# Probabilities times V for four query tiles in one slot instead of a quarter in each of four

## Chip, cores and metric

One core of one Trainium2 chip. The metric is the device time of one execution in microseconds (us).

## What is computed

`x` is [8, 1024, 512] in float32: eight batches ("b") of 1024 tokens. The block has two halves. The first is attention on the normalised input, with a residual:

```python
xn = layernorm(x)
qk = (xn @ W_qk + b_qk).reshape(b, s, 8, 64, 2);  q, k = qk[..., 0], qk[..., 1]
v = (xn @ W_v + b_v).reshape(b, s, 8, 64)
attn = softmax(einsum('bihd,bjhd->bhij', q, k) * 64 ** -0.5)
o = einsum('bhij,bjhd->bihd', attn, v).reshape(b, s, 512)
x = x + (layernorm(o @ W_out + b_out) * gamma + beta + xn) * 2 ** -0.5
```

The second half normalises x again, mixes each token with the one before it, and computes `sigmoid(xr @ W_r.T) * (relu(xk @ W_k.T) ** 2 @ W_v.T)`, which is added to x. The change touches only the line with `attn` times `v`.

## The kernel before, in words

Two passes stand one behind the other: `attention_pass` (L60 to L629), which leaves the attention output in DRAM (`o_scratch`), and `mix_pass` (from L632), which does the rest in chunks of 512 tokens. The change lies in the attention pass. Each engine has its own hand-written program, and semaphores tie them together; a `wait_ge` holds everything behind it on its engine.

The attention pass runs a loop over the batches (seven turns of `entry(b, False)` and one last `entry(B - 1, True)`). A batch is a row of slots, n = 0 to 69 (`LAST_SLOT` is 70). Slot n belongs to head h = n // 8 and has r = n % 8. There are 8 heads with 8 query tiles of 128 tokens each, so slots 0 to 63 each make the scores of one tile, and the slots behind them finish. In slot n, TensorE (PE) does in this order:

- `scores(b, n)` (L503): 4 matmuls of 512 columns into one of two score buffers `ps_scores`, each two PSUM banks wide. It waits until the exponential of tile n - 2 has read the buffer (`exp_done`), and at r = 0 for the head's q and k.
- in slots 55 to 58 and 62 to 65 (`XHAT_TURNS`), except in the last batch, the transposes of one tile of the next batch's normalised input, `turn_xhat` (L458), through `ps_misc`. They wait for the readers of what ps_misc held before (`misc_free_of_qk`, `misc_free_of_xhat`).
- in the first slots of a batch the products for V, `project_v` (L497).
- at r = 3 `spread_inv` (L544): transposes of the reciprocal row sums of the head before, through `ps_misc`. At n = 66 that of the last head, through the bank of `ps_turnA`, behind that slot's products.
- `turn_probs(b, n - 2)` (L518): eight transposes of the probabilities of tile n - 2, four into `ps_turnA` and four into `ps_turnB`. Each half waits until the bank was copied out for the tile before (`turnA_stored`, `turnB_stored`).
- `p_at_v` (L528): probabilities times V. Four query tiles make a "quad"; quad number `quad` covers the tiles 4 * quad to 4 * quad + 3 and needs all four turned. For each of the 8 key tiles (jt) there are two matmuls of 64 output rows and 256 columns, one per half of the array's columns; two tiles share one of them. They accumulate in `ps_o`, whose left half takes the head's first quad (q2 = 0) and its right half the second (q2 = 1). The before-kernel calls it in every slot from n = 6 on with part = (n - 6) % 4 and does 2 of the 8 key tiles each time. The first part waits for the turned probabilities, and at q2 = 0 for `o_done`, that VectorE has read `ps_o` for the head before.
- `project_qk` (L464): pieces of the q and k projection of the next head, 4 matmuls at r = 7, 0 and 1, 6 matmuls at r = 3 and 4, none at r = 2, 5 and 6. The piece at r = 3 waits (L603) until `inv_cols` was copied out of `ps_misc`. Heads 6 and 7 have none in slots 55 to 58; the next batch's first head is projected in slots 59, 60 and 65.

VectorE (DVE) does in slot n: the row maximum of the scores of tile n (L330), at r = 1 the reciprocal of the row sums and its widening (L337, L339), at r = 2 the rests of k and q (L290, L296), at r = 5 that of k and at r = 6 that of q, in the xhat slots `xT_lo` (L283), then the copy of `ps_turnB` (tile n - 2) into `probsT` (L357), in slots 38 to 45 statistics of the next batch (L261), in slots 52, 53 and the xhat slots `normalise` (L277), and last, at r = 5 and h >= 1, the product `oT = ps_o * inv_cols` of the head before (L376), which waits for `pv_done`.

ScalarE (ACT) does in slot n: the exponential of tile n - 1 (L433, with its row sum), at r = 2 and 5 the copies of q and k (L402, L403), in the xhat slots `xT_hi` (L396), the copy of `ps_turnA` (tile n - 2) into `probsT` (L445), and at r = 3 the copy of the spread reciprocals into `inv_cols` (L411); for the last head this stands at n = 66. At a batch's end PE waits for that copy (L624) and for `turnB_stored` (L625) before its loop turns.

`probsT` has room for two quads. SyncE's queue copies k between partition halves (L186, L187), stores oT (L192) and loads the next x.

Of the kernel before, what the change touches and what calls it, by code (L numbers as in the profile page):

```python
# [27 lines left out]
TT = T // P  # L28
# [11 lines left out]
QUAD = 4  # L40
# [19 lines left out]
def attention_pass(nc, x, w_qk, b_qk, w_v, b_v, w_out, w_r, w_out_raw, stage, o_scratch, ln1_stats, ident):  # L60
    with ExitStack() as ctx:
# [3 lines left out]
        def sem(name):  # L65
            return ctx.enter_context(nc.semaphore(name))
# [84 lines left out]
        turnA_stored = sem("turnA_stored")  # L151
        turnB_stored = sem("turnB_stored")
# [5 lines left out]
        o_done = sem("o_done")  # L158
# [6 lines left out]
        with nc.Block() as block:  # L165
# [291 lines left out]
            def _(pe):  # L457
                def turn_xhat(b, t, turned):  # L458
                    pe.wait_ge(xhat_done, 8 * b + t + 1)
                    for k in range(KC):  # L460
                        ins = pe.transpose(turned[:, k, :], xhat[t % 2][:, k * P:(k + 1) * P], ident[:, :])
                    ins.then_inc(xhatT_done, 1)
# [13 lines left out]
                def misc_free_of_qk(b, h, half):  # L476

                    pe.wait_ge(qk_hi_done, 16 * b + 2 * h + half + 1)
                    pe.wait_ge(qk_lo_done, 16 * b + 2 * h + half + 1)

                def misc_free_of_xhat(b, t):
                    pe.wait_ge(xT_hi_done, 8 * b + t + 1)
                    pe.wait_ge(xT_lo_done, 8 * b + t + 1)
# [13 lines left out]
                def project_v(b, t):  # L497
                    prods = [(xt, w, kc) for kc in range(KC) for xt, w in ((xT_lo, wv_hi), (xT_hi, wv_lo), (xT_hi, wv_hi))]
                    for i, (xt, w, kc) in enumerate(prods):
                        ins = pe.matmul(v_banks[t], xt[:, kc, t * P:(t + 1) * P], w[:, kc, :], start=(i == 0), stop=(i == 11))  # L500
                    ins.then_inc(v_done, 1)

                def scores(b, n):  # L503
                    h, r = n // TT, n % TT
                    if r == 0:
                        pe.wait_ge(qk_lo_done, 16 * b + 2 * h + 2)
                        pe.wait_ge(k_copied[h % 2], 128 * b + 32 * (h // 2) + 32)
                    if n >= 2:
                        pe.wait_ge(exp_done, 64 * b + n - 1)
                    tile = slice(query_tile(r) * P, (query_tile(r) + 1) * P)  # L510
                    for half in range(2):
                        cols = slice(half * HALF, (half + 1) * HALF)
                        for i, k in enumerate((k_lolo, k_hihi)):
                            ins = pe.matmul(ps_scores[n % 2][:, cols], q_hilo[h % 2][:, tile], k[h % 2][:, cols],  # L514
                                            start=(i == 0), stop=(i == 1))
                    ins.then_inc(scores_done, 1)
# [8 lines left out]
                            ins = pe.transpose(ps[:, j, :], probs[m % 3][:, (first + j) * P:(first + j + 1) * P], ident[:, :])  # L525
                        ins.then_inc(done, 1)

                def p_at_v(b, quad, part):  # L528

                    h, q2 = quad // 2, quad % 2  # L530
                    if part == 0:
                        pe.wait_ge(turnA_stored, 64 * b + QUAD * quad + QUAD)
                        pe.wait_ge(turnB_stored, 64 * b + QUAD * quad + QUAD)
                        if q2 == 0 and h >= 1:
                            pe.wait_ge(o_done, 8 * b + h)
                    for jt in (2 * part, 2 * part + 1):
                        for half in range(2):
                            ins = pe.matmul(ps_o[half * DH:(half + 1) * DH, q2 * 2 * P:(q2 + 1) * 2 * P],  # L538
                                            v[:, jt, h * DH:(h + 1) * DH], probsT[:, quad % 2, jt, half, :],
                                            start=(jt == 0), stop=(jt == TT - 1))  # L540
                    if part == 3 and q2 == 1:
                        ins.then_inc(pv_done, 1)

                def spread_inv(b, h, turned=ps_misc[:, :]):  # L544
# [7 lines left out]
                def entry(b, last):  # L552
                    for n in range(LAST_SLOT):
                        h, r = n // TT, n % TT
                        if n == 0:
                            project_v(b, 0)
                            project_v(b, 1)
                        if n < SLOTS:
                            scores(b, n)
                        if not last and n in XHAT_TURNS:  # L560
                            t = XHAT_TURNS.index(n)
                            if t == 0:
                                misc_free_of_qk(b, HEADS - 1, 1)
                            elif t == 4:
                                misc_free_of_qk(b + 1, 0, 0)
                            else:
                                misc_free_of_xhat(b + 1, t - 1)
                            turn_xhat(b + 1, t, misc4)
                        for t in range(TT):
                            if V_SLOTS[t] == n and n > 0:  # L570
                                if t in (2, 4, 5, 6, 7):

                                    pe.wait_ge(v_stored, 8 * b + (1 if t == 2 else t))
                                project_v(b, t)
                        if r == 3 and 1 <= h < HEADS:
                            if h < HEADS - 1:
                                misc_free_of_qk(b, h + 1, 0)
                            elif last:
                                misc_free_of_qk(b, h, 1)
                            else:  # L580
                                misc_free_of_xhat(b + 1, 3)
                            spread_inv(b, h - 1)
                        if n == 2:
                            pe.wait_ge(v_stored, 8 * b + 3)
                        if 2 <= n < SLOTS + 2:
                            turn_probs(b, n - 2)
                        if n == 6:
                            pe.wait_ge(v_stored, 8 * b + TT)
                        if n >= 6:
                            p_at_v(b, (n - 6) // QUAD, (n - 6) % QUAD)  # L590

                        if h < HEADS - 1:
                            if n == 0:
                                misc_free_of_qk(b, 0, 1)
                                project_qk(b, 1, 0, 0, 4)
                            if r == 0:
                                project_qk(b, h + 1, 0, 4, 8)
                            if r == 1:
                                project_qk(b, h + 1, 0, 8, 12)
                            if r == 3:  # L600
                                misc_free_of_qk(b, h + 1, 0)
                                if h >= 1:
                                    pe.wait_ge(inv_stored, 8 * b + h)  # L603
                                project_qk(b, h + 1, 1, 0, 6)
                            if r == 4:
                                project_qk(b, h + 1, 1, 6, 12)
                            if r == 7 and h < HEADS - 2:
                                misc_free_of_qk(b, h + 1, 1)
                                project_qk(b, h + 2, 0, 0, 4)
                        if not last:  # L610

                            if n == 59:
                                pe.wait_ge(inv_stored, 8 * b + h)
                                project_qk(b + 1, 0, 0, 0, 6)
                            if n == 60:
                                project_qk(b + 1, 0, 0, 6, 12)
                            if n == 65:
                                misc_free_of_xhat(b + 1, TT - 1)
                                project_qk(b + 1, 0, 1, 0, 12)
                        if n == SLOTS + 2:  # L620
                            pe.wait_ge(turnA_stored, 64 * b + SLOTS)
                            spread_inv(b, HEADS - 1, turnA_bank)
                        if n == LAST_SLOT - 1 and not last:
                            pe.wait_ge(inv_stored, 8 * b + HEADS)  # L624
                            pe.wait_ge(turnB_stored, 64 * b + SLOTS)  # L625

                with pe.Fori(0, B - 1) as b:
                    entry(b, False)
                entry(B - 1, True)  # L629


# [525 lines left out]
```

## Time and profile before

| | |
|---|---|
| time, median of 3 runs | 3000.94 us (3000.56 to 3002.95) |
| span of the profiled execution, first to last instruction | 2998.2 us |
| PE busy | 2890.0 us, 96% |
| weight loads (beside PE) | 2168.0 us, 72% |
| DVE busy | 2068.8 us, 69% |
| ACT busy | 1572.7 us, 52% |
| DMA, hardware queue | 14.6% of 16 engines |
| instructions | 44311 |

The span is that of one execution; its whole time was not taken apart from the three runs, whose median lies 2.7 us above it. PE's busy time counts from the start of a matmul to its modelled end, and matmuls overlap, so a busy PE may still be waiting for an array that drains. A line of the timeline is one instruction, or several of one kind in a row (xN); the number in brackets is idle time before it and what ended it.

### The profile page before, as it was taken

The numbers are of one execution on the slowest core, as the hardware profiler recorded it, in microseconds if no ns is written. First come the engines' busy times: TensorE is split into PE (matmuls) and PEld (weight loads), VectorE is DVE, ScalarE is ACT, GpSimd is POOL, SyncE is SP. The second block draws the span as 40 slices with busy tenths as digits, with TensorE's granted clock in tenths as the row PEclk, the third lists the DMA queues.
The fourth block names the chain that finished last, engine by engine and source line by source line (L and its number), as shares of the span: only waits on it lengthen the run. The fifth ranks groups of instructions, "written<-read, shape, count | busy, mean of one in ns | idle before, by whom it ended". The sixth has DMA issues, their size and how long they took to land. (4 is left out here: it accounts for less than half of the span.)

```text
span 2998.2 us, 44311 instructions
## 1 busy us (share of the span) xinstructions
PE 2890.0 (96%) x16432; PEld 2168.0 (72%) x16432; DVE 2068.8 (69%) x2885; ACT 1572.7 (52%) x2553; POOL 278.5 (9%) x227
## 2 busy tenths in 40 slices
PE   7999999999999999999999999999969999999999
PEld 5777777777777777777777777777747777777777
DVE  5667566656756665675666566666668898989896
ACT  3555455455535555554555455455545555555453
POOL 2000000000000000000000000000013333233332
PEclk9999999999999999999999999999979999999999
DMA  3101110111011111111110111111131111111110
GB/s 102 50 22 26 33 47 22 33 32 40 22 37 36 33 34 32 30 32 26 47 24 23 39 40 25 23 29 50 26 98 57 70 59 66 63 63 66 59 70 29
DMA packets 61407, 128.62 MB, mean 43 GB/s; under 512 B 8464, under 2 KB 8464, under 8 KB 61200
## 3 DMA queue, kind: packets, MB, share of 16 engines
q1 hardware_dynamic: 61200, 125.86, 14.6%
q8 instruction: 130, 2.13, 0.3%
q14 instruction: 77, 0.63, 0.1%
HBM read 58.73 MB, written 33.55 MB: 31 GB/s over the span
## 5 line engine op out<-in xcount | busy, mean ns | idle before, releaser
L330 DVE TENSOR_REDUCE neg_max<-ps_scores 128x1 f32<-128x1024 f32 x512 | 625.0, 1221 | 601.5 <-PE ps_scores L514 601.4
L433 ACT ACTIVATE probs<-ps_scores,neg_max 128x1024 f32<-128x1024 f32 x512 | 571.3, 1116 | 219.3 <-DVE neg_max L330 218.9
L445 ACT ACTIVATE probsT<-ps_turnA 128x512 f32<-128x512 f32 x512 | 305.4, 597 | 572.2 <-PE ps_turnA L525 569.6
L538 PE MATMUL ps_o<-probsT,v 128*64 128x256 f32 x4096 | 551.3, 391 | 4.0 <-DVE oT L376 2.5
L514 PE MATMUL ps_scores<-k_lolo,q_hilo 128*128 128x512 f32 x1024 | 423.9, 414 | 1.0 <-DMA k_lolo<-k_lolo 1.0
L514 PE MATMUL ps_scores<-k_hihi,q_hilo 128*128 128x512 f32 x1024 | 401.5, 392 | 0.0
L538 PEld LDWEIGHTS ps_o<-probsT,v 128*64 128x64 f32 x4096 | 251.0, 136 | 164.9 <-issue 83.7
L357 DVE COPY probsT<-ps_turnB 128x512 f32<-128x512 f32 x512 | 350.7, 685 | 10.9 <-PE ps_turnB L525 4.8
L525 PE MATMUL ps_turnB<-ident,probs 128*128 128x128 f32 x2048 | 308.1, 273 | 0.5
L525 PE MATMUL ps_turnA<-ident,probs 128*128 128x128 f32 x2048 | 306.5, 272 | 0.0
L525 PEld LDWEIGHTS ps_turnA<-ident,probs 128*128 128x128 f32 x2048 | 250.6, 140 | 53.7 <-issue 0.8
L514 PEld LDWEIGHTS ps_scores<-k_lolo,q_hilo 128*128 128x128 f32 x1024 | 191.9, 187 | 113.7 <-issue 77.7
L525 PEld LDWEIGHTS ps_turnB<-ident,probs 128*128 128x128 f32 x2048 | 238.9, 141 | 3.2 <-DVE probsT L357 2.3
L471 PE MATMUL ps_misc<-xT_hi,wqk_lo 128*128 128x512 f32 x508 | 219.9, 433 | 1.5 <-DVE xT_lo L283 1.5
L514 PEld LDWEIGHTS ps_scores<-k_hihi,q_hilo 128*128 128x128 f32 x1024 | 192.5, 188 | 33.7
L471 PE MATMUL ps_misc<-xT_lo,wqk_hi 128*128 128x512 f32 x508 | 205.9, 405 | 0.0
L471 PE MATMUL ps_misc<-xT_hi,wqk_hi 128*128 128x512 f32 x508 | 205.7, 405 | 0.0
L237 POOL TENSOR_TENSOR rstd<-mean_var,eps 128x8 f32<-128x8 f32 x8 | 1.6, 201 | 1810.6 <-DVE mean_var L265 1810.6
L402 ACT ACTIVATE q_hilo<-ps_misc,bqk 64x512 fp32r<-64x512 f32 x127 | 86.9, 684 | 146.6 <-PE ps_misc L471 145.7
L471 PEld LDWEIGHTS ps_misc<-xT_hi,wqk_lo 128*128 128x128 f32 x508 | 95.8, 189 | 77.2 <-issue 60.8
L1060 PE MATMUL bank<-mix_wv_hi,act_lo 128*128 128x512 f32 x256 | 104.6, 409 | 28.6 <-DVE act_lo L867 20.8
L290 DVE SCALAR_TENSOR_TENSOR k_lolo<-ps_misc,bqk,k_hihi 64x512 fp32r<-64x512 f32 x127 | 96.1, 757 | 41.3 <-ACT k_hihi L403 37.5
(175 smaller groups left out, 4602.5 us busy)
## 6 DMA issues: line engine op xcount, KB each, us to landing
stage<-in_L_attn_x_dram SPq DMA_DIRECT2D x32, 512.0 KB, 4.3
k_hihi<-k_hihi SPq DMA_DIRECT2D x64, 256.0 KB, 2.9
k_lolo<-k_lolo SPq DMA_DIRECT2D x64, 256.0 KB, 3.9
o_scratch<-oT SPq DMA_DIRECT2D x128, 128.0 KB, 3.1
stage<-o_scratch SPq DMA_DIRECT2D x16, 1024.0 KB, 5.6
xc<-in_L_attn_x_dram SPq DMA_DIRECT2D x16, 1024.0 KB, 5.2
out_dram<-gate SPq DMA_DIRECT2D x64, 256.0 KB, 2.1
probsT<-in_L_attn_W_qk_dram SPq DMA_DIRECT2D x4, 512.0 KB, 8.4
```

What stands on the lines that cost most here:

```text
L237: pool.tensor_tensor(rstd[:, :], mean_var[:, :, 1], eps[:, :], ALU.add).then_inc(eps_done, 1)
L290: dve.scalar_tensor_tensor(k_lolo[i][DH:P, cols], ps[DH:P, :], bqk[DH:P, h:h + 1], f32(k_hihi[i][DH:P, cols]), ALU.add, ALU.subtract).then ...
L330: dve.tensor_reduce(neg_max[:, h % 2, r:r + 1], ps_scores[n % 2][:, :], AX_X, ALU.max, negate=True).then_inc(max_done, 1)
L357: dve.tensor_copy(probsT[:, m // QUAD % 2, 4:8, m % 2, m % QUAD // 2 * P:(m % QUAD // 2 + 1) * P], ps_turnB[:, :, :]).then_inc(turnB_store ...
L402: act.activation(q_hilo[i][0:DH, cols], ps[0:DH, :], ACT.Identity, bias=bqk[0:DH, h:h + 1])
L433: act.activation(probs[m % 3][:, :], ps_scores[m % 2][:, :], ACT.Exp, bias=neg_max[:, m // TT % 2, m % TT:m % TT + 1], accum_out=row_sum[: ...
L445: act.activation(probsT[:, m // QUAD % 2, 0:4, m % 2, m % QUAD // 2 * P:(m % QUAD // 2 + 1) * P], ps_turnA[:, :, :], ACT.Copy).then_inc(tu ...
L471: ins = pe.matmul(ps[:, :], w[:, kc, h, :, :].rearrange("p s d -> p (s d)"), xt[:, kc, cols], start=(n == 0), stop=(n == 11))
L514: ins = pe.matmul(ps_scores[n % 2][:, cols], q_hilo[h % 2][:, tile], k[h % 2][:, cols], start=(i == 0), stop=(i == 1))
L525: ins = pe.transpose(ps[:, j, :], probs[m % 3][:, (first + j) * P:(first + j + 1) * P], ident[:, :])
L538: ins = pe.matmul(ps_o[half * DH:(half + 1) * DH, q2 * 2 * P:(q2 + 1) * 2 * P], v[:, jt, h * DH:(h + 1) * DH], probsT[:, quad % 2, jt, hal ...
L1060: ins = pe.matmul(out, a[:, kc, a_cols], b[:, kc, b_cols], start=(i == 0), stop=(i == len(prods) - 1))
```

## The change

The four calls of `p_at_v` for a quad become one, in the slot of the first: all 8 key tiles, 16 matmuls, at n = 6, 10, 14, ... 66. The waits stay the same and stand ahead of it. `pv_done` now rises in slot r = 2 instead of r = 5. No other instruction is added, removed or moved, and no buffer changes. At n = 66 `spread_inv` now stands behind the whole of the last quad.

```diff
-                def p_at_v(b, quad, part):
+                def p_at_v(b, quad):
 
                     h, q2 = quad // 2, quad % 2
-                    if part == 0:
-                        pe.wait_ge(turnA_stored, 64 * b + QUAD * quad + QUAD)
-                        pe.wait_ge(turnB_stored, 64 * b + QUAD * quad + QUAD)
-                        if q2 == 0 and h >= 1:
-                            pe.wait_ge(o_done, 8 * b + h)
-                    for jt in (2 * part, 2 * part + 1):
+                    pe.wait_ge(turnA_stored, 64 * b + QUAD * quad + QUAD)
+                    pe.wait_ge(turnB_stored, 64 * b + QUAD * quad + QUAD)
+                    if q2 == 0 and h >= 1:
+                        pe.wait_ge(o_done, 8 * b + h)
+                    for jt in range(TT):
                         for half in range(2):
                             ins = pe.matmul(ps_o[half * DH:(half + 1) * DH, q2 * 2 * P:(q2 + 1) * 2 * P],
                                             v[:, jt, h * DH:(h + 1) * DH], probsT[:, quad % 2, jt, half, :],
                                             start=(jt == 0), stop=(jt == TT - 1))
-                    if part == 3 and q2 == 1:
+                    if q2 == 1:
                         ins.then_inc(pv_done, 1)
...
-                        if n >= 6:
-                            p_at_v(b, (n - 6) // QUAD, (n - 6) % QUAD)
+                        if n >= 6 and (n - 6) % QUAD == 0:
+                            p_at_v(b, (n - 6) // QUAD)
```

## Rows read from the trace of the kernel before

**Rows 1.** The page, part 1: busy us, share of the span, instructions.
```profile
PE 2890.0 (96%) x16432; PEld 2168.0 (72%) x16432; DVE 2068.8 (69%) x2885; ACT 1572.7 (52%) x2553; POOL 278.5 (9%) x227
```

**Rows 2.** Table of stretches, one batch: us, busy us per engine, PE clock, DMA.
```profile
340.00:610.00 270.00, 266.95 (x1634) 194.48 (x1633) 170.36 (x226) 143.82 (x242) 1.83 (x2) 1.00 0.13 32
```

**Rows 3.** The page, part 5: the products of probabilities and V on PE.
```profile
L538 PE MATMUL ps_o<-probsT,v 128*64 128x256 f32 x4096 | 551.3, 391 | 4.0 <-DVE oT L376 2.5
```

**Rows 4.** Timeline, slots 5 and 6 of a head: start us, us, engine, line.
```profile
731.38 0.39 PE L514 MATMUL ps_scores<-k_lolo,q_hilo 128*128 128x512 f32 x1
...
732.49 1.23 DVE L330 TENSOR_REDUCE neg_max<-ps_scores 128x1 f32<-128x1024 f32 x1 [2.57 <-PE ps_scores L514]
...
732.73 0.60 PE L525 MATMUL ps_turnB<-ident,probs 128*128 128x128 f32 x4
...
733.25 1.08 PE L538 MATMUL ps_o<-probsT,v 128*64 128x256 f32 x8
733.75 0.76 DVE L290 SCALAR_TENSOR_TENSOR k_lolo<-ps_misc,bqk,k_hihi 64x512 fp32r<-64x512 f32 x1
...
734.54 0.69 DVE L357 COPY probsT<-ps_turnB 128x512 f32<-128x512 f32 x1
734.60 0.39 PE L514 MATMUL ps_scores<-k_hihi,q_hilo 128*128 128x512 f32 x1
...
735.26 0.69 DVE L376 TENSOR_TENSOR oT<-ps_o,inv_cols 128x512 f32<-128x512 f32 x1
...
736.26 0.44 PE L538 MATMUL ps_o<-probsT,v 128*64 128x256 f32 x2
```

**Rows 5.** Timeline of PE, a slot without such a block.
```profile
337.28 0.60 PE L525 MATMUL ps_turnB<-ident,probs 128*128 128x128 f32 x4
...
337.95 0.40 PE L471 MATMUL ps_misc<-xT_lo,wqk_hi 128*128 128x512 f32 x1
```

**Rows 6.** Timeline, slot 3 of a head and the start of slot 4.
```profile
721.94 0.50 PE L514 MATMUL ps_scores<-k_lolo,q_hilo 128*128 128x512 f32 x1
...
724.65 0.59 ACT L411 ACTIVATE inv_cols<-ps_misc 128x512 f32<-128x512 f32 x1
...
725.50 0.50 PE L471 MATMUL ps_misc<-xT_hi,wqk_lo 128*128 128x512 f32 x1
...
726.99 0.39 PE L514 MATMUL ps_scores<-k_lolo,q_hilo 128*128 128x512 f32 x1
```

**Rows 7.** Timeline of DVE, slot 56.
```profile
534.39 0.68 DVE L283 TENSOR_TENSOR xT_lo<-ps_misc,xT_hi 128x512 fp32r<-128x512 f32 x1
...
535.59 0.54 DVE L277 TENSOR_SCALAR xhat<-stage,mean_var,rstd 128x512 f32<-128x512 f32 x1
```

**Rows 8.** Timeline, the start of slot 46's block.
```profile
496.20 0.67 DVE L376 TENSOR_TENSOR oT<-ps_o,inv_cols 128x512 f32<-128x512 f32 x1
...
497.02 1.08 PE L538 MATMUL ps_o<-probsT,v 128*64 128x256 f32 x8 [0.36 <-DVE oT L376]
```

**Rows 9.** Timeline, slot 66 to the next batch's first matmul.
```profile
569.72 1.08 PE L538 MATMUL ps_o<-probsT,v 128*64 128x256 f32 x8
...
570.73 0.66 PE L549 MATMUL ps_turnA<-ident,inv_wide 128*128 128x128 f32 x4
...
571.32 2.81 PE L538 MATMUL ps_o<-probsT,v 128*64 128x256 f32 x24
571.42 0.60 ACT L411 ACTIVATE inv_cols<-ps_turnA 128x512 f32<-128x512 f32 x1 [0.22 <-PE ps_turnA L549]
...
576.45 0.47 PE L500 MATMUL ps_turnA<-wv_hi,xT_lo 128*128 128x512 f32 x1 [2.33 <-issue]
```

**Rows 10.** Stretches behind the attention pass (columns as in rows 2), and PE's timeline there.
```profile
2177.00:2180.00 3.00, 0.38 (x4) 0.00 (x0) 0.69 (x1) 0.00 (x0) 0.00 (x0) 1.00 0.21 49
2189.00:2194.00 5.00, 5.00 (x13) 3.73 (x13) 0.92 (x5) 0.00 (x0) 0.00 (x0) 0.50 1.05 397
...
2188.66 0.76 PE L1060 MATMUL bank<-mix_wout_hi,o_lo 128*128 128x512 f32 x1 [11.28 <-DVE o_lo L838]
```

## The prediction

> **What bounds the kernel now.** First the page's busy times: TensorE (PE) is busy for 2890 of 2998.2 us, VectorE (DVE) for 69%, ScalarE (ACT) for 52% [rows 1]. Then the table of stretches: in one batch of the attention pass PE is busy for 266.95 of 270 us at a granted clock of 1.00 [rows 2]. So the attention pass (7 x 269 us and a shorter last batch) is bound by PE, and PE's slots set the beat. But a busy PE need not be doing work: the timeline shows what a block of products of probabilities and V costs beside its columns. Last I read who is how late behind PE in the slots where the block now disappears: DVE's chain there [rows 4] and ACT's [rows 6]. I call a slot by r = n mod 8.
>
> **A quarter block and its switch.** With a block, the second matmul of the next slot starts 734.60 - 732.73 = 1.87 us after the first transpose into turnB [rows 4]; in a slot without one, 337.95 - 337.28 = 0.67 us later [rows 5]. A block costs PE 1.20 us. Its work is less: the stretch of 24 records takes 2.81 us, one of 8 takes 1.08 [rows 9], so a further pair of records (the two halves run side by side) takes 1.73 / 8 = 0.216 us, and a block's four pairs 0.86. The other 0.34 us is paid for going into the 64-column form and out again. The page has 4096 records [rows 3], 8 to a block: 512 blocks, 128 quads. A quad in one go costs PE 1.20 + 12 x 0.216 = 3.79 us, not 4.80: 1.01 less. If PE alone counted, that were 128 x 1.01 = 129 us, less a little at the batch ends.
>
> The work now lies in slots r = 2 and r = 6 (2.59 us longer), and slots 0, 1, 3, 4, 5, 7 are 1.20 us shorter. What used to pass under their blocks comes into view, slot by slot.
>
> **Slots 5 and 6.** Let slot 5 begin at 0 (731.38). DVE: row maximum 1.11 to 2.34, k rest 2.37 to 3.13, copy of turnB 3.16 to 3.85, the product into oT (L376) 3.88 to 4.57 [rows 4]. This chain starts from the slot's own scores and does not get shorter. PE's next product block writes the ps_o that L376 reads, and waits for it (o_done); today it starts at 4.88, just after, so nobody is seen to wait. Without the block in slot 5, PE would reach it at 1.35 (turnB) + 0.67 + 3 x 0.23 + 0.44 + 0.52 = 3.67. It can't start before 4.57 + 0.15 = 4.72; the 0.15 is from the place where this wait already shows, 496.87 to 497.02 [rows 8]. So of 1.20 us only 0.16 are gained. What is queued behind the wait on PE is the whole block and slot 7; DVE and ACT catch up meanwhile. In slots 45 and 53 of a batch a further DVE instruction stands ahead of L376, so the wait shows today already (slot 46's block is the one in [rows 8]), and the gain is 0.
>
> **Slot 3.** The projection's second half overwrites ps_misc, which ACT reads for inv_cols (L411). ACT ends it at 725.24, 3.30 us after the slot's start; the projection starts at 3.56 today [rows 6], with the block in between. Without it PE is ready at about 2.4, but waits until 3.30 less 0.08 (the transposes of inv_wide no longer wait for the q rest of slot 2) plus 0.15: 3.37. Gain 0.19, with a shorter start-up 0.21, not 1.20. Slots 4, 7, 0 and 1 keep their whole 1.20: maximum and copy (1.23 + 0.69) fit into slots of 2.7 us or more, and the scores' round trip (2.4 us to the end of maximum and exponential behind the scores) fits into two slots.
>
> **A head.** From the block of r = 2 to that of r = 6: +2.59 - 0.21 - 1.20 - 0.16 = +1.02 us. From r = 6 to r = 2: 2.59 - 3 x 1.20 = -1.01. A head is unchanged. Per batch, quads 0 to 12 (the first gap is of the cheap kind): -6 x 1.01 + 6 x 1.02 + 2 x 0.16 = +0.4 us.
>
> **Slots 55 to 66, next batch's xhat.** These slots have no projection, and each turns a tile of xhat through ps_misc. PE without the block needs 0.92 + 0.44 + 0.87 = 2.23 us; DVE needs 1.14 + 0.60 + 0.60 + 0.57 = 2.9 (maximum, xT_lo, copy, normalise [rows 7]), and some 0.57 more in slot 57. Over 55 to 57 DVE falls 9.3 - 6.7 = 2.6 us behind; the two score banks absorb part. Following xT_lo to the next transpose I get a wait of 0.45 in slot 57 and 1.1 in slot 58: +0.6 net between slots 55 and 59 instead of -1.0. Slots 59 and 60: -0.2 and -1.2. Slot 61 stores k and q rests, so its DVE chain is 0.8 longer and sets the next block's start today already: 0. Slots 63 to 65: transpose, ACT's xT_hi, DVE's xT_lo, next transpose is a round trip of some 2.1 us, beside a PE need of 1.31 in slots 64 and 65, so the three give back only 0.9 of 3.6. With the two blocks' extra 2.59 each (quads 12 and 14): +0.6 - 1.4 + 5.2 - 0.9 = +3.5. Bounds: 0 lost to these waits gives -0.8; all of DVE's lag and of the round trips in view gives +4.5. I take +3.5, from following the chain.
>
> **The batch's end.** Today a quarter block at 569.72 is followed by the transposes of inv_wide at 570.73, ACT copies them from 571.42 to 572.02, and three quarters (571.32 to 574.13) run meanwhile; PE's stream waits for that copy (L624), turns the loop, and the next batch's first matmul is at 576.45, with 2.33 us idle on "issue" [rows 9]. That is 4.43 us after the copy. Now the transposes stand behind the whole quad: copy's end at 3.29 + 0.31 + 0.66 + 0.04 + 0.60 = 4.9 us after the block's start, not 2.3. If the loop's turn runs from the wait's release, the next batch starts 2.6 us later; if it runs from the last matmul (2.3 us after it), 4.9 + 2.3 against 6.7: 0.5 later. I take 2.6, as the idle time has no other releaser and the sequencer is ahead of the array.
> By the Trainium skill (Runtime: NRT & Kernel Launch, Instruction fetch mechanics) a taken branch whose target is not held forces a fetch before execution goes on. By that rule the turn's price hangs on when the branch is reached, and the 2.6 stands; no run here shows the fetch itself yet.
>
> **Sum.** A batch with a successor: +0.4 + 3.5 + 2.6 = +6.5 us less roundings, say +6.3; seven of them 44 us. The last batch has no xhat and no loop turn: its slots 55 to 61 keep most of their gain and the end is 0.5 later; 0 within 3 us. The mix pass is untouched. Against the profiled span 2998.2 this is 3042; the medians lie 2.7 above the span (3000.94), so 3045.
>
> **Rivals.**
> 1. PE alone sets the time (faster). The waits of slots 3 and 6 don't bind: then 7 x (1.04 + 0.99) more is gained in each of 8 batches, about 110 us: 2935; and with the xhat slots and the ends free as well, 2872. It decides at one point: if L376 were over 3.5 us after slot 5 begins. Against it: four DVE instructions behind the scores sum to 3.4 us whatever PE does [rows 4].
> 2. The clock falls. PE is idle at the seven batch ends for over 4 us instead of 2.3. After the attention pass comes an idle time of 11.28 us: the clock is 1.00 in its first 3 us, and 0.50 when PE resumes, with 13 matmuls in 5 us [rows 10], 0.38 us each instead of 0.23: 2 us lost each time. 14 us, to 3059. For it: the longer idle time; against: it is nearer to 2.3 than to 11.
> The Trainium skill (TensorE: Matmul & The Clock Gate, Why this matters for your kernels) tells to avoid idle gaps between bursts of matmuls for this reason. By that rule this edit is worse than the sum says; the trace agrees only in that 11.28 us were too long.
> 3. The price at xhat and at the ends is half of mine: 3045 - 7 x (1.5 + 1.5) = about 3024.
> 4. It balances out: the two waits a little shorter (0.3 us each) give 3045 - 8 x 7 x 0.6 = 3011, and with rival 3 below 3000. This is the "same" case.
>
> **How the numbers follow.** Forecast 0.57, rival 2 0.15, rival 3 0.10, rival 4 0.08, rival 1 0.10. A measurement of this kernel can tell 0.2%, 6 us, from no change. The range goes from rival 4 (3011, taken as 3012) to rival 2 with turns of the loop 2 us dearer still (3059 + 7 x 2 = 3073, taken as 3075). Faster 0.11, same 0.07, slower 0.82.
>
> **What would show it.** In the new profile PE busy falls by far more than the span changes; L538 has 128 groups of 32 records. PE waits appear: the block of r = 6 for L376 (about 1 us, 7 per batch), the projection of slot 3 for L411 (about 1 us, 7 per batch), transposes of xhat for L283 in slots 57, 58, 64, 65. The gap between batches rises from 2.3 to over 4 us. Wrong if PE's idle time in an ordinary head is under 1.5 us, if the first matmul of a batch follows its last one as closely as today, or if the granted clock drops inside the attention pass.

## The result, and the profile after

The changed kernel takes 3056.44 us (median of 4 runs, 3054.43 to 3057.02), the kernel before 3000.75 us in the same comparison. The ratio is 1.0181, 95% interval 1.0166 to 1.0195: 55.7 us slower. The forecast was 3045, from 3012 to 3075.

The page of the changed kernel: the span, then part 1 (busy us, share, instructions), then two groups of part 5 (busy, mean ns of one, idle before and its releaser).

```profile
span 3054.2 us, 44311 instructions
...
PE 2808.2 (92%) x16432; PEld 2224.8 (73%) x16432; DVE 2079.4 (68%) x2885; ACT 1557.1 (51%) x2553; POOL 278.6 (9%) x227
...
L537 PE MATMUL ps_o<-probsT,v 128*64 128x256 f32 x4096 | 470.3, 382 | 15.7 <-DVE oT L376 14.8
...
L471 PE MATMUL ps_misc<-xT_hi,wqk_lo 128*128 128x512 f32 x508 | 216.4, 426 | 50.9 <-ACT inv_cols L411 45.0
```

The instructions are the same in number. PE is busy 81.8 us less than in [rows 1] and the products 81.0 us less than in [rows 3], though the edit leaves out nothing but switches; and the span is 56 us longer. So PE's work became cheaper and its idle time grew by more than the whole saving. The list of waits says where. Its columns: engine, line, what it waited for, us in total, times, longest.

```profile
PE ps_misc L471 <- ACT inv_cols L411: 45.0, 55, 0.8
PE ps_turnB L525 <- DVE probsT L357: 28.6, 49, 0.6
PE ps_turnA L500 <- issue: 28.0, 6, 4.8
...
PE ps_misc L461 <- DVE xT_lo L283: 19.2, 28, 0.9
...
PE ps_o L537 <- DVE oT L376: 14.8, 48, 0.8
...
PE ps_misc L461 <- DVE q_hilo L296: 9.2, 7, 1.4
PE ps_misc L471 <- DVE xT_lo L283: 5.9, 8, 1.5
```

Read it by the counts. 55 is seven heads in each of seven batches and six in the last: the projection of slot 3, which waits for inv_cols. 48 are six heads in eight batches (49 with one more place): the block of r = 6, which waits for the copy of turnB and then for the product into oT (0.6 and 0.3 us a place). 28 is four xhat slots in seven batches. 7 is slot 62. 6 is the loop's turn: seven batches have a successor, but the seventh leaves the loop instead of turning it. Idle time is counted from the modelled end of the matmul before, so a sum of these times is less than what the waits cost.

The timeline of the changed kernel, slots 3 to 7 of the head that [rows 6] and [rows 4] show before (start us, duration us, engine, line):

```profile
738.93 0.50 PE L514 MATMUL ps_scores<-k_lolo,q_hilo 128*128 128x512 f32 x1
...
740.83 0.60 PE L525 MATMUL ps_turnB<-ident,probs 128*128 128x128 f32 x4
...
741.52 0.59 ACT L411 ACTIVATE inv_cols<-ps_misc 128x512 f32<-128x512 f32 x1
...
742.26 0.47 PE L471 MATMUL ps_misc<-xT_hi,wqk_lo 128*128 128x512 f32 x1 [0.83 <-ACT inv_cols L411]
...
743.73 0.40 PE L514 MATMUL ps_scores<-k_lolo,q_hilo 128*128 128x512 f32 x1
...
746.91 0.40 PE L514 MATMUL ps_scores<-k_lolo,q_hilo 128*128 128x512 f32 x1
...
750.08 0.69 DVE L357 COPY probsT<-ps_turnB 128x512 f32<-128x512 f32 x1
...
750.80 0.69 DVE L376 TENSOR_TENSOR oT<-ps_o,inv_cols 128x512 f32<-128x512 f32 x1
750.83 0.66 PE L525 MATMUL ps_turnB<-ident,probs 128*128 128x128 f32 x4 [0.59 <-DVE probsT L357]
...
751.64 3.67 PE L537 MATMUL ps_o<-probsT,v 128*64 128x256 f32 x32 [0.15 <-DVE oT L376]
...
755.24 0.50 PE L514 MATMUL ps_scores<-k_lolo,q_hilo 128*128 128x512 f32 x1
```

Slot 3 lasts 743.73 - 738.93 = 4.80 us against 5.05 before: 0.25 gained where a quarter block of 1.20 has left. Slot 4 lasts 3.18 against 4.39: the whole 1.20. From the start of slot 5 to the block of r = 6 it is 751.64 - 746.91 = 4.73 us against 4.88: 0.15 gained of 1.20. The block takes 755.24 - 751.64 = 3.60 us to the next scores.

The batch's end in the changed kernel's timeline, and below it two stretches (length, busy us by engine, granted clock, DMA):

```profile
580.49 3.67 PE L537 MATMUL ps_o<-probsT,v 128*64 128x256 f32 x32
...
584.09 0.66 PE L548 MATMUL ps_turnA<-ident,inv_wide 128*128 128x128 f32 x4
584.78 0.60 ACT L411 ACTIVATE inv_cols<-ps_turnA 128x512 f32<-128x512 f32 x1 [2.81 <-PE ps_turnA L548]
...
589.30 0.77 PE L500 MATMUL ps_turnA<-wv_hi,xT_lo 128*128 128x512 f32 x1 [4.55 <-issue]
```

```profile
588.00:596.00 8.00, 6.70 (x17) 5.28 (x18) 0.69 (x1) 0.00 (x0) 0.00 (x0) 0.57 0.35 92
596.00:604.00 8.00, 8.00 (x36) 6.48 (x35) 3.14 (x3) 2.28 (x4) 0.00 (x0) 1.00 0.00 0
```

The copy of inv_cols ends 4.89 us after the block began, where [rows 9] give 2.30. The next batch follows 3.92 us after the copy (4.43 in [rows 9]), 8.81 after the block began instead of 6.73. And PE resumes at the lower of its two clock levels: 0.57 on average over 8 us, 17 matmul starts, where the next 8 us hold 36 at 1.00.

The turn in [rows 9] is the slowest of its kernel. From the end of the copy to the next batch's first matmul the six turns before take 3.69 to 4.43 us, 3.90 on average, and those of the changed kernel 3.90 to 4.21, 4.03 on average. The trace has a record of the branch itself, on PE's sequencer (ns shortest/median/longest, first and last start in us), in the kernel before:

```profile
L627 PEldq COMPARE_BRANCH  x7: 83/3521/4151, 303.0 to 1918.5; - x7
```

and in the changed one:

```profile
L626 PEldq COMPARE_BRANCH  x7: 83/3698/3924, 308.6 to 1974.5; - x7
```

The one of 83 ns leaves the loop. The first of the kernel before starts 0.1 us after the copy of its batch ends (302.86), though three quarters of the last quad still run then; in the changed kernel the record at 585.5 starts 0.1 us after the copy (585.38) too, and PE has nothing left to run.

The starts in PE's timeline cut each batch in four. "Block" stands for the first product of probabilities and V in a slot. The numbers are us, added up over the seven batches with a successor; the forecast's are those ahead of its "less roundings":

| from, to | forecast difference | before | changed | difference |
|---|---|---|---|---|
| first V matmul, block of slot 6 | 0 | 275.7 | 287.8 | +12.1 |
| block of slot 6, block of slot 54 | +2.8 | 1271.7 | 1270.9 | -0.8 |
| block of slot 54, block of slot 66 | +24.5 | 295.2 | 321.4 | +26.2 |
| block of slot 66, next first V matmul | +18.2 | 41.6 | 58.7 | +17.1 |

Together they are +54.6 of the 55.7 us. The first row is the clock's. No wait was added in these slots. Behind each of the loop's six turns the stretch takes 39.2 us before and 40.5 to 42.0 in the changed kernel; in the first batch, which has no turn ahead of it, it takes 40.4 in both. For the batches that start at 576.45 and 589.30 its end is (the kernel before, then the changed one)

```profile
615.66 1.08 PE L538 MATMUL ps_o<-probsT,v 128*64 128x256 f32 x8
```

```profile
631.32 3.67 PE L537 MATMUL ps_o<-probsT,v 128*64 128x256 f32 x32
```

39.21 and 42.02 us after the start.

### The profile page after: what moved, and what is told of

Same layout as the page of the kernel before. It is cut to its first block and busy times, and to the rows that moved or that the text cites. A ratio compares the mean times of both kernels' runs of the same rounds, so it can differ in the third digit from the quotient of the medians.

```text
span 3054.2 us, 44311 instructions
## 1 busy us (share of the span) xinstructions
PE 2808.2 (92%) x16432; PEld 2224.8 (73%) x16432; DVE 2079.4 (68%) x2885; ACT 1557.1 (51%) x2553; POOL 278.6 (9%) x227
## 5 line engine op out<-in xcount | busy, mean ns | idle before, releaser
L537 PE MATMUL ps_o<-probsT,v 128*64 128x256 f32 x4096 | 470.3, 382 | 15.7 <-DVE oT L376 14.8
L537 PEld LDWEIGHTS ps_o<-probsT,v 128*64 128x64 f32 x4096 | 303.9, 137 | 150.2 <-issue 39.3
L357 DVE COPY probsT<-ps_turnB 128x512 f32<-128x512 f32 x512 | 351.2, 686 | 14.3 <-PE ps_turnB L525 4.0
L525 PE MATMUL ps_turnB<-ident,probs 128*128 128x128 f32 x2048 | 310.6, 274 | 29.2 <-DVE probsT L357 28.6
L471 PE MATMUL ps_misc<-xT_hi,wqk_lo 128*128 128x512 f32 x508 | 216.4, 426 | 50.9 <-ACT inv_cols L411 45.0
L471 PE MATMUL ps_misc<-xT_hi,wqk_hi 128*128 128x512 f32 x508 | 205.0, 404 | 0.0
L471 PE MATMUL ps_misc<-xT_lo,wqk_hi 128*128 128x512 f32 x508 | 204.4, 402 | 0.0
L471 PEld LDWEIGHTS ps_misc<-xT_hi,wqk_lo 128*128 128x128 f32 x508 | 96.2, 189 | 76.5 <-issue 49.9
L1059 PE MATMUL bank<-mix_wout_hi,o_lo 128*128 128x512 f32 x256 | 103.2, 403 | 23.5 <-DVE o_lo L837 12.0
```

Source lines behind the costliest of these rows:

```text
L357: dve.tensor_copy(probsT[:, m // QUAD % 2, 4:8, m % 2, m % QUAD // 2 * P:(m % QUAD // 2 + 1) * P], ps_turnB[:, :, :]).then_inc(turnB_store ...
L471: ins = pe.matmul(ps[:, :], w[:, kc, h, :, :].rearrange("p s d -> p (s d)"), xt[:, kc, cols], start=(n == 0), stop=(n == 11))
L1059: ins = pe.matmul(out, a[:, kc, a_cols], b[:, kc, b_cols], start=(i == 0), stop=(i == len(prods) - 1))
```

## The experiments

Each run was timed in turn with the kernel before. Theory A is the prediction's: a slot that loses its quarter block is held by the chain behind it, if there is one. Theory B: a quad in one go costs the same everywhere. Theory C: PE saves everywhere, and the loss is at the batch ends alone.

| run | what it is | us | ratio to before, 95% |
|---|---|---|---|
| after | the change | 3056.4 | 1.0181 (1.0166 to 1.0195) |
| e1_even | quads 0, 2, ... 10 in one go | 2957.3 | 0.985 (0.9833 to 0.9866) |
| e2_odd | quads 1, 3, ... 11 | 3058.2 | 1.0181 (1.0164 to 1.0198) |
| e3_xhat | quads 12, 13, 14 | 3032.4 | 1.0097 (1.0077 to 1.0118) |
| e4_tail | quad 15 | 3031.3 | 1.0093 (1.0076 to 1.011) |
| e5_tail_first | after, inv_wide turned ahead of the last quad | 3025.9 | 1.0079 (1.0063 to 1.0096) |
| e6_inv_first | after, inv_cols copied first in slot 3 | 3006.0 | 1.001 (1.0001 to 1.002) |
| e7_vector | after, new order on DVE in slot 5 | 3015.3 | 1.0043 (1.0026 to 1.006) |
| e8_both | e6 and e7 | 2965.4 | 0.9878 (0.9861 to 0.9894) |
| e9b_heads_both | e8, quads 12 to 15 in quarters | 2913.5 | 0.9704 (0.9688 to 0.972) |
| e10b_before_orders | before, with the new orders | 3008.5 | 1.002 (1.001 to 1.0029) |
| e11_not_slot61 | e9b, slot 61 in its old order | 2914.7 | 0.9701 (0.9687 to 0.9714) |
| e12_last_quad_too | e11 and quad 15 as in e5 | 2910.8 | 0.9692 (0.9679 to 0.9705) |

### The change in four parts

```diff
+WHOLE = [0, 2, 4, 6, 8, 10]      # e2: [1, 3, ... 11]   e3: [12, 13, 14]   e4: [15]
...
-                        if n >= 6:
-                            p_at_v(b, (n - 6) // QUAD, (n - 6) % QUAD)
+                        if n >= 6:
+                            quad, part = (n - 6) // QUAD, (n - 6) % QUAD
+                            if quad not in WHOLE:
+                                p_at_v(b, quad, part, part + 1)
+                            elif part == 0:
+                                p_at_v(b, quad, 0, 4)
```

`p_at_v(b, quad, part, end)` does the key tiles 2 * part to 2 * end - 1.

Even quads. 

> Only quads 0, 2, 4, 6, 8 and 10 of each batch are made in one go (slots 6, 14, ... 46); all others in quarters as before. Theory A (each slot that loses its quarter is held by the chain that stands behind it): here slots 7, 0 and 1 are shortened, where nothing is late, and slot 5 keeps its quarter, so every one of the 48 quads saves the full 1.01 us: 3001 - 48 = 2952 us. Theory B (a quad in one go costs the same everywhere, +55.7 us / 128 = +0.43 us): 3001 + 21 = 3022 us. Theory C (PE alone would save everywhere, and the whole loss is at the batch ends): 2952 us as A.

Odd quads. 

> Only quads 1, 3, 5, 7, 9 and 11 in one go (slots 10, 18, ... 50), the others in quarters. Here slots 3, 4 and 5 are shortened. Theory A: of 3.6 us the waits of slot 3 (inv_cols) and of slot 6 (product into oT) take back about 2, so each of 48 quads costs +1.0 us: 3001 + 48 = 3049 us. Theory B: 3022 us. Theory C: 2952 us.

Measured: 45.9 us faster and 55.0 us slower than the 3003.2 us of the kernel before in these runs. The kind of edit and the number of quads are the same, and the sign turns with the slots that become short. B and C are out. The page's group of products falls by the same amount in both, from 551.3 to 519.6 us busy:

```profile
L539 PE MATMUL ps_o<-probsT,v 128*64 128x256 f32 x4096 | 519.6, 388 | 4.0 <-DVE oT L377 2.5
```

```profile
L539 PE MATMUL ps_o<-probsT,v 128*64 128x256 f32 x4096 | 519.6, 387 | 14.8 <-DVE oT L377 14.8
```

The first is the even quads', the second the odd quads'. What differs is the list of waits; that of the odd quads begins

```profile
PE ps_misc L472 <- ACT inv_cols L412: 39.9, 48, 0.8
PE ps_turnB L526 <- DVE probsT L358: 28.4, 48, 0.6
```

and in that of the even quads neither line stands. The odd quads cost 7 us more than expected: 1.15 us each, not 1.0. In the changed kernel the whole block of r = 6 hides what DVE still has to make up after slot 5; here slot 6 has only a quarter, and slot 7 is 0.13 us longer than before (4.17 against 4.04): its turnB transposes start at 696.37, 0.06 us after DVE's copy ends.

In the trace of the even quads the stretch from the block of slot 6 to that of slot 54 is 6.03 us shorter per batch, 1.01 a quad; in that of the odd ones it is 6.61 longer, 1.10 a quad.

Quads 12 to 14. 

> Only quads 12, 13 and 14 in one go (slots 54, 58 and 62), where the next batch's xhat is turned; the others, the last one too, in quarters. Theory A: +3.5 us in each of the seven batches that have a successor, about -1 in the last: 3001 + 24 = 3025 us. Theory B: 24 quads x 0.43 = +10: 3011 us. Theory C: -24 us, 2977 us. No change of the clock in any of them.

Measured +29.2 us, theory A's side but 5 us more. From the block of slot 54 to that of slot 66 it is 3.7 us in each of seven batches, 26.0, and +0.6 in the last, where -1 was expected. The waits for xT_lo are 19.2 us at 28 places, as in the changed kernel. (One of its four executions took 14.9 ms and is not in the ratio.)

Quad 15. 

> Only quad 15 of each batch in one go, so that the spread of the reciprocals stands behind the whole quad; all others in quarters. Theory A: the loop turns 2.6 us later and the clock falls to 0.5 at the turn, some 2.3 us more, at six turns: 3001 + 29 = 3030 us; idle time before a batch's first matmul 4.5 us instead of up to 2.3. If the loop's turn did not hang on that copy: within 5 us of 3001. Theory B: 8 x 0.43, 3004 us.

Measured +28.1 us. Its list of waits has the loop's turn at 28.9 us for six, where the kernel before has 10.8 (its rows: "PE ps_turnA L500 <- issue: 10.8, 6, 2.3"):

```profile
PE ps_turnA L501 <- issue: 28.9, 6, 5.1
```

So 18 us are idle time, and some 10 us are left for the clock. The trace has 11.9 us for it: from a batch's first V matmul to the block of slot 6 the six batches behind a turn take 40.6 to 42.0 us instead of 39.2. The stretch in which PE resumes is granted 0.79 on average over 8 us.

```profile
582.00:590.00 8.00, 6.54 (x22) 5.29 (x23) 0.69 (x1) 0.00 (x0) 0.00 (x0) 0.79 0.29 89
```

The four parts add up to -45.9 + 55.0 + 29.2 + 28.1 = +66.4; the whole change is +55.7. In the heads 0.7 us a batch (6.61 - 6.03 + 0.1), 5.5 in eight, is taken back where both kinds are whole: the odd quads' excess, which the even quads' blocks hide. The rest was not traced; executions of the kernel before alone lie 3.4 us apart in these runs.

### The changed kernel with one cause taken away

```diff
+                        if n == SLOTS + 2:
+                            pe.wait_ge(turnA_stored, 64 * b + SLOTS)
+                            spread_inv(b, HEADS - 1, turnA_bank)
                         if n >= 6:
...
-                        if n == SLOTS + 2:
-                            pe.wait_ge(turnA_stored, 64 * b + SLOTS)
-                            spread_inv(b, HEADS - 1, turnA_bank)
```

> The changed kernel, but at slot 66 the transposes of inv_wide stand ahead of the last quad instead of behind it. If the loop's turn and the clock's fall come from their place: 3056 - 28 = 3028 us, idle time at a batch's end back under 2.5 us, granted clock 1.00 over the attention pass. If the length of the merged block itself delays the turn: 3056 us.

Measured 30.5 us less than the changed kernel. The turn's idle time is 13.1 us for six (28.0 in the changed kernel), and the clock did not fall: the stretch from the first V matmul to the block of slot 6 is back at 39.2 us behind all six turns, with every quad in one go. So the fall comes from the longer idle time and not from the bundling. The turn itself did not get shorter (3.94 to 4.38 us from the copy): the block runs beside it.

```diff
+                        if r == 3 and 1 <= h < HEADS:
+                            store_inv(b, h)
                         if 2 <= n < SLOTS + 2:
                             m = n - 2
                             act.wait_ge(turnA_done, 64 * b + m + 1)
...
-                        if r == 3 and 1 <= h < HEADS:
-                            store_inv(b, h)
```

> The changed kernel, but ScalarE copies inv_cols at r = 3 ahead of its copy of turnA instead of behind it. Theory A: the projection's wait in slot 3 falls from about 0.8 to 0.1 or 0.2 us at 55 places: 3056 - 40 = 3016 us (3008 to 3024). If PE's idle time there is not on the path: 3056 us.

Measured 50.5 us less. The wait at L471's place is gone from the list altogether, so nothing of it was left where 0.1 to 0.2 us were expected: 50.5 / 55 = 0.92 us a place. The heads' stretch says the same: 5.55 us less per batch for six places.

```diff
+                def first(n):
+                    return n % TT == 5 and TT < n < SLOTS
...
+                        if first(n):
+                            copy_turnB(b, n)
                         if h < HEADS - 1:
                             if r in QK_STORES:
...
-                        if 2 <= n < SLOTS + 2:
+                        if 2 <= n < SLOTS + 2 and not first(n):
...
-                        if r == 5 and h >= 1:
+                        if h >= 1 and r == (4 if 2 * h - 1 in WHOLE else 5):
```

`copy_turnB` holds the wait and the copy of L357.

> The changed kernel, but VectorE at r = 5 copies turnB ahead of the k rest, and makes the product into oT at r = 4, where its quad is done since slot 2. Theory A: the block of r = 6 no longer waits for either: 1.0 us at 48 places and more in slots 45 and 53: 3056 - 52 = 3004 us (2996 to 3014). If something else is just behind (the exponential, the copy of turnA): less than half of that, 3030 us or more.

Measured 41.2 us less, 11 short of the expected 52. Both waits of r = 6 are gone, and the heads gave more than expected, 7.2 us a batch or 57 in eight; but slots 54 to 66 took 12 back, because slot 61 got worse. The next batch's xhat transposes wait for the q rest of that slot, which now stands behind the copy:

```profile
825.15 0.65 PE L470 MATMUL ps_misc<-ident,xhat 128*128 128x128 f32 x4 [1.87 <-DVE q_hilo L297]
...
827.33 4.57 PE L547 MATMUL ps_o<-probsT,v 128*64 128x256 f32 x32
```

The block of 32 records takes 4.57 us here instead of 3.67, and the stretch shows why, a clock of 0.66. So it is in five of the seven batches, where slots 54 to 66 take 2.2 us more than in the changed kernel; in the other two the same idle time (1.86 us at 282.99) is followed by a block of 3.67 and the price is 0.6.

```profile
825.00:830.00 5.00, 4.85 (x28) 3.48 (x30) 3.01 (x4) 2.29 (x4) 0.00 (x0) 0.66 0.01 3
```

> Both orders of the two runs before in the changed kernel. Theory A: they add, 3056 - 92 = 2964 us (2950 to 2985). If the one wait moves into the place of the other: 3004 us or more.

Measured 2965.4: 91.0 us less than the changed kernel, and 50.5 + 41.2 = 91.7. They add, in the heads too (5.55 + 7.2 us a batch, and 12.8 in this run); neither wait moves into the place of the other.

### A version that beats both

> Quads 0 to 11 of each batch in one go, quads 12 to 15 in quarters as before (so the xhat slots and the batch's end are untouched), and both new orders (inv_cols ahead of the copy of turnA at r = 3; copy of turnB ahead of the k rest and the product into oT one slot earlier at r = 5). Theory A: 96 quads save 1.01 us each less some 0.1 us of waits left in a head's slots 3 and 6: 3001 - 97 + 10 = 2914 us (2900 to 2930). If freed time only meets the next wait: 2955 us or more.

Measured 2913.5 us, 3.0% faster than the kernel before and 4.7% faster than the changed one. PE is as busy as in [rows 1], 96%, with 92 us less to do:

```profile
span 2912.7 us, 44311 instructions
...
PE 2797.9 (96%) x16432; PEld 2194.3 (75%) x16432; DVE 2077.8 (71%) x2885; ACT 1556.2 (53%) x2553; POOL 278.8 (10%) x227
```

> The kernel before, all quads in quarters, with the new order of inv_cols at r = 3 and the copy of turnB ahead of the k rest at r = 5 (the product into oT stays at r = 5, as its quad ends in that slot). Theory A: the quarters hide both, so the orders alone are worth nothing: 3001 us, within 5. If the orders pay by themselves: under 2990 us.

Measured 5.7 us slower than before, just outside what was expected and clear of no change. The orders are worth nothing where the quarters stand, and cost in slot 61: its list of waits has a line that the kernel before has not, 0.6 us in each of seven batches. One fall of the clock behind a turn adds 1.5 us in the profiled run.

```profile
PE ps_misc L470 <- DVE q_hilo L297: 4.5, 7, 0.6
```

> As the run of quads 0 to 11 in one go with both orders, but slot 61 keeps its old order on VectorE (k rest and q rest ahead of the copy of turnB). Theory A: the next batch's xhat transposes of slot 62 wait for that q rest, so the new order cost 0.6 us there in each of seven batches: 2913 - 4 = 2909 us (2905 to 2913), and the wait for it in the trace goes from 0.7 to 0.2 us.

```diff
-                    return n % TT == 5 and TT < n < SLOTS
+                    return n % TT == 5 and TT < n < 7 * TT
```

A miss: 2914.7 us, no gain. The wait itself behaved: the line for q_hilo goes from 9.5 us at 14 places to 5.0 at 7. Slots 54 to 66 gained 0.6 us in each of seven batches, 4.2, as forecast. But in the profiled run PE resumes slower after the loop's turn. The stretch behind the second turn, first in this run, then in the one without the edit:

```profile
556.00:560.00 4.00, 4.00 (x12) 3.10 (x11) 0.69 (x1) 0.00 (x0) 0.00 (x0) 0.57 0.47 139
```

```profile
554.00:558.00 4.00, 3.79 (x16) 3.12 (x17) 0.69 (x1) 0.00 (x0) 0.00 (x0) 1.00 0.70 192
```

This run had such a fall at five of six turns, the other at two. A fall costs 1.5 us: from the first V matmul to the block of slot 6 it is 40.76 us with one and 39.22 without, in both runs. Three more took back the whole gain; whether they are chance or come from the edit wasn't tried.

> As the run before, and quad 15 in one go as well, with the transposes of inv_wide ahead of it. Theory A: one switch of 0.34 us less per batch, 2909 - 3 = 2906 us; if the loop's turn is now hidden beside the long block as well, up to 10 us less than that. If long blocks at the end delay the turn: 2915 us or more.

Measured 2910.8 us, 4 us less than the run before, whose interval overlaps with it, and its profiled run had one fall of the clock less. The turn was not hidden beside the longer block.

## Why the prediction was right

**A quarter block and its switch.** 0.34 us was the right size. In e1 nothing else changes, and from the block of slot 6 to that of slot 54 six quads save 6.03 us in every batch, 1.01 each as forecast. The whole program's 45.9 us are 0.96 a quad; in its profiled run the clock fell at two turns, 1.5 us each, and in that of the kernel before at none.

**Slots 5 and 6.** The chain and the time were right: the block could not start before 4.72 us, and starts at 4.73. One wait was missing. Slot 6's transposes into turnB need the copy of turnB, which ends 0.7 us ahead of the product into oT, so PE first waits 0.6 us for the copy and then only 0.3 for the product, not 1 us for the product. The sum holds, since both hang on the same chain of DVE. And such places are six a batch, not seven. Taking both waits away (e7) gives the time back, except in slot 61.

**Slot 3.** Right: 0.21 us of gain forecast, 0.25 found. e6 shows 0.92 us a place.

**A head.** "A head is unchanged" holds: -0.1 us a batch against +0.4, as a sum of -6.0 for the even quads and about +6 for the odd ones (+6.6 alone). This is the step that mattered: the saving and the new waits are nearly equal, and only the parts alone show both.

**Slots 55 to 66.** Right, and close: +3.5 us a batch was forecast, 3.7 measured, in the changed kernel and in e3. The last batch adds 0.6.

**The batch's end.** The place was right and e5 confirms it. The choice between the two readings was right too: the branch's record starts when the wait for the copy is over, not behind the last matmul, and the turn takes the same with a block beside it or without. At the place shown the start is 2.08 us later and not 2.6, but only because the turn of [rows 9] is the slowest of its kernel; over the six turns it is 2.7. One count was off. The prediction has "seven of them", but the loop turns six times; the seventh time it leaves, where the next start is only 0.8 us later. Together 17.1 us against 18.2.

**Rival 2, the clock.** This is what the forecast lacked, and why 55.7 came where 44 was said. The forecast stood at 1.00 throughout and gave the fall a chance of 0.15 and a price of 14 us. It happened at all six turns and cost 12.1. It is also one of the prediction's own signs of being wrong, "if the granted clock drops inside the attention pass"; the other two did not come (PE idles 1.58 us in an ordinary head of 30.07, a little over the 1.5 named). So the chains and the turn are right, and the clock's part of the forecast is wrong.

From the first V matmul of one batch to that of the next it was 845.75 - 576.45 = 269.30 us before, and is 867.72 - 589.30 = 278.42: 9.1 us more where the ledger has 6.3, and 2.8 of them are the clock's.

```profile
867.72 0.77 PE L500 MATMUL ps_turnA<-wv_hi,xT_lo 128*128 128x512 f32 x1 [4.72 <-issue]
```

The argument against the fall ("it is nearer to 2.3 than to 11") was weak: an idle time between one that did no harm and one that did says nothing of which side it falls on. Without the clock the table above has 42.5 us where the ledger has 44: 3.6 too much for the heads and 1.1 for the ends, 1.7 too little for slots 55 to 66, and 1.4 taken off as roundings. That these nearly cancel is luck, but each is small.

**Rivals 1, 3 and 4.** Rival 1 fell by e2: PE alone would have saved there. But its saving in the heads (about 110 us) is close to what e9b reaches there once the two chains are moved: 12.9 us a batch, 102 in eight. Rival 3 asked for half the price at xhat and at the ends; e3 and e4 show its full size. Rival 4 asked for waits in slots 3 and 6 that are 0.3 us shorter; the gains there are 0.25 and 0.15 us where 0.21 and 0.16 were forecast.

## What to carry to other kernels

Work that is spread over slots covers other engines' chains, even where the list of waits shows none: before bundling it, write down for every slot that loses it when the next reader's release comes, from that slot's own start. Where a release is late, first move what stands ahead of it on its own engine (here two moves on DVE and one on ACT turned +55.7 us into -37), and leave the pieces where they are in slots whose chain can't be shortened (that made it -89). Try the change by classes of place: six of the sixteen quads of a batch were a gain of 46 us, hidden behind a loss of 55 from six others. And where a change lengthens an idle time of TensorE, give the clock a term of its own: here it was 12 of 56 us.

## What the runs showed of the hardware

Going from 128x128 matmuls to the two side-by-side 64-column ones and back costs PE 0.34 us by the timeline before and by e1 (6.03 us / 6 quads / 3 switches), for blocks of 8 records and of 32. That it is the change of form, and not something else at a block's two ends, was not taken apart.

The granted clock fell to the lower level at all 30 turns of the changed kernel, e4, e6, e7 and e8, with 4.5 to 5.1 us of idle time, and PE then lost 1.3 to 2.8 us. Near 2 us the length does not decide. It fell in e9b after 1.89 and 2.26 us and not after 2.31 and 2.23; in e7 it fell after the same 1.87 us in slot 62 in five batches and not in two; at the turns of the kernel before and of e5, with up to 2.33 and 2.37 us, it never fell. Within each kernel the same slots run ahead of these gaps, so they do not decide alone either. What does is open.

A loop's turn of PE took 3.69 to 4.43 us in the kernel before, 3.90 to 4.21 in the changed one and 3.94 to 4.38 in e5, from the end of the copy it waits for to its next matmul. Nearly all of it is the record of the branch (3.4 to 4.15 us before; those of DVE and ACT in the same loop are 0.06 and 0.05 us). The record starts when the sequencer is past its last wait (what it does from there on the trace does not tell), with matmuls still under way or not, so work queued behind that wait's release covers a part: with a block of 3.6 us beside it 2.2 us of idle time a turn remain (e5, 13.1 for six), with nothing 4.7 (28.0).
